# Flamingo block on one core: the split chain moves from VectorE to GpSimd, both norms' scales become one chain, and the second product's last tiles move one step on

## The reference, cut to what matters

```python
x = x + tanh(g_xattn) * xattn(layernorm(x), ctx, Wq, Wkv, Wout, bout)
x = x + tanh(g_ffn)   * ffn(layernorm(x), ln1_g, ln1_b, w1, b1, ln2_g, ln2_b, w2, b2)
# ffn: h = layernorm(x)*ln1_g + ln1_b ; h = bitlinear(h, w1, b1) ; h = gelu(h)
#      h = layernorm(h)*ln2_g + ln2_b ; h = bitlinear(h, w2, b2)
# bitlinear: the row is rounded to 8 bits with scale 127/max|row|,
#      w is rounded to -1, 0 or 1 with scale 1/mean|w|, then x @ w.T + b
```

## Time and profile before

| | |
|---|---|
| median of 3 executions | 404.12 us (401.83 to 404.73) |
| profiled execution | 403.77 us, span 401.9 us |
| VectorE, TensorE, ScalarE, GpSimd busy | 82%, 77%, 69%, 55% of the span |
| mean granted TensorE clock | 0.945 |

### The profile page before, as it was taken

The page is one execution under the profiler, slowest core; times in us unless marked ns, Lnnn a source line. Parts: engine busy times, 40 slices in busy tenths (PEclk is TensorE's granted clock), DMA queues, the critical chain, the costliest instruction groups (busy, mean ns, idle before and its releaser), DMA issues.

```text
span 401.9 us, 5821 instructions
## 1 busy us (share of the span) xinstructions
PE 309.3 (77%) x1690; PEld 189.8 (47%) x1690; DVE 328.1 (82%) x794; ACT 277.6 (69%) x446; POOL 220.9 (55%) x118
## 2 busy tenths in 40 slices
PE   2887586969797978888888888888879675848465
PEld 2675344435555555545454546464636342515143
DVE  0489237979999999999999999999999995968781
ACT  1214456869787878796969696969696967879340
POOL 4021163949292929393948484848484757565500
PEclk9999698969999999999999999999999996969688
DMA  7774413336282829191919282828170717252625
GB/s 226 231 238 172 131 52 81 104 58 133 74 208 76 214 66 223 55 229 59 229 60 213 76 195 95 182 106 174 62 155 31 140 44 114 72 111 73 157 55 155
DMA packets 97687, 51.56 MB, mean 128 GB/s; under 512 B 86536, under 2 KB 88769, under 8 KB 97655
## 3 DMA queue, kind: packets, MB, share of 16 engines
q1 hardware_dynamic: 96758, 51.14, 49.9%
q10 hardware_dynamic: 896, 0.04, 0.1%
HBM read 21.78 MB, written 8.41 MB: 75 GB/s over the span
## 4 chain that ended last, share of the span: by engine, by line
DVE 41%; PE 35%; issue 9%; POOL 7%; ACT 3%; DMA 3%; DVEq 0%; POOLq 0%; SPq 0%; ACTq 0%
DVE y L683 10%; PE bank_f L951 8%; POOL rstd L320 6%; PE slot_c L913 5%; DVE res L733 5%; DVE h L642 5%; DVE amax L650 5%; PE slot_a L939 4%; DVE amax L687 3%; PE bank_q L892 3%; PE slot_b L939 3%; DMA c_in<-in_ctx 3%; DVE x L599 3%; DVE parts L585 2%; PE slot_a L936 2%
## 5 line engine op out<-in xcount | busy, mean ns | idle before, releaser
L336 POOL TENSOR_TENSOR y<-u,g_bc 128x1024 f32<-128x1024 f32 x64 | 150.2, 2368 | 27.8 <-DVE parts L585 25.4
L320 POOL TENSOR_TENSOR rstd<-var,half_neg 128x8 f32<-128x8 f32 x18 | 29.5, 1641 | 99.1 <-DVE var L724 88.1
L683 DVE TENSOR_TENSOR y<-y,slot_c 128x1024 f32<-128x1024 f32 x64 | 77.6, 1212 | 5.3 <-PE slot_c L913 5.3
L687 DVE TENSOR_REDUCE amax<-y 128x1 f32<-128x1024 f32 x64 | 78.1, 1220 | 2.2
L427 ACT ACTIVATE q<-y,s 128x1024 f16<-128x1024 f32 x64 | 69.8, 1139 | 9.9 <-DVE s L714 9.8
L454 ACT ACTIVATE junk<-u,usum 128x1024 bf16<-128x1024 f32 x64 | 73.7, 1151 | 1.2
L951 PE MATMUL bank_f<-w2T,q2T 128*128 128x256 f16 x512 | 68.1, 281 | 2.0 <-DVE res L733 2.0
L892 PE MATMUL bank_q<-wvo,ctxT 128*128 128x256 f32 x240 | 64.6, 401 | 0.0
L951 PEld LDWEIGHTS bank_f<-w2T,q2T 128*128 128x128 f16 x512 | 51.4, 101 | 16.6 <-DVE res L733 2.9
L913 PE MATMUL slot_c<-ln_rows,rows 128*128 128x512 bf16 x128 | 41.5, 408 | 16.9 <-DVE y L683 8.4
L418 ACT ACTIVATE q<-h,s 128x256 f16<-128x256 f32 x64 | 27.3, 496 | 37.6 <-DVE s L674 37.5
(11 more groups left out here) (115 smaller groups left out, 407.9 us busy)
## 6 DMA issues: line engine op xcount, KB each, us to landing
c_in<-in_ctx SPq DMA_DIRECT2D x16, 512.0 KB, 3.3
x_in<-in_x SPq DMA_DIRECT2D x16, 512.0 KB, 4.2
out<-res SPq DMA_DIRECT2D x32, 256.0 KB, 2.6
y<-in_L_ffn_w SPq DMA_DIRECT2D x2, 1024.0 KB, 9.6
u<-in_L_xattn_Wkv SPq DMA_DIRECT2D x1, 1024.0 KB, 6.7
u<-in_L_xattn_Wout SPq DMA_DIRECT2D x1, 1024.0 KB, 10.4
q2T<-q SPq DMA_TRANSPOSE x64, 3.3
g_bc<-in_L_ffn_ln_g SPq DMA_DIRECT2D x1, 512.0 KB, 4.3
```

The source lines that it names most:

```text
L320: nc.gpsimd.tensor_tensor(rstd[:, :, :], var[:, :, :], half_neg[:, :, :], ALU.pow) \
L336: nc.gpsimd.tensor_tensor(y[:, k % 2, t, :], u[:, t, :], g2_bc[:, :], ALU.mult).then_inc(gain2_done, 1)
L683: nc.vector.tensor_tensor(line, line, slot_c[:, :], ALU.add).then_inc(y_done, 1)
L687: nc.vector.tensor_reduce(amax2[:, t:t + 1], y[:, k % 2, t, :], AX.X, ALU.max, apply_absolute_value=True).then_inc(amax2_done, 1)
```

## The change

- `variance`, `deviations` and `split` leave VectorE's program and stand in GpSimd's. GpSimd's body begins with `deviations` and the five steps of `split` and ends with `variance(i)` and `root(i + 1)`. `rstd` gets a second buffer. GpSimd's wait for the split steps ahead of its gains goes away with that, and only tile 3's `gain` stays one body later.
- `first` and `second` become one chain `scales` of six instructions over both norms (128x8 where it was 128x4), at the end of the body, with nothing between its dependent steps.
- `join` of set i+2 is cut into its four steps, which stand between `row` and `row_max` of tiles 0 and 1.
- `rows` is doubled. `take_rows` stands behind the first `quantise`.
- The second product's tiles 2 and 3 and their `final` run one body later; tiles 0 and 1 run behind `hidden(3)`.
- The second half of attention writes slot_b and is run at the end of the body before; TensorE turns the first half of the next context at the body's start.
- Body 0 has an order of its own, with `shift_first(1)` ahead of most of its products.

```diff
+                def variance(k):
+                    wait(pool, square_done, T * k + T)
+                    wait(pool, std_done, i + 2)
+                    wait(pool, split_steps, split_count(i))
+                    nc.gpsimd.tensor_scalar(stat[:, 2, :], usum[:, :], -1.0 / H, None, ALU.mult)
+                    nc.gpsimd.tensor_scalar(var[:, 1, :], usq[:, :], 1.0 / float(H) ** 3, LN_EPS,
+                                            ALU.mult, ALU.add).then_inc(var2_done, 1)
+                def split(n):
+                    if n == 0:
+                        wait(pool, std_done, min(i + 2, S + 2))
+                        wait(pool, join_steps, 3 * min(i + 2, S))
+                        wait(pool, scales_ready, scales_after(i - 1))
+                        wait(pool, rows_done, i + 1)
...
                 if -1 <= i <= S:
-                    root()
-                    wait(pool, split_steps, split_count(i))
+                    deviations()
+                if -1 <= i <= S + 1:
+                    for n in range(5):
+                        split(n)
...
                 if live(i - 1):
-                    gain(i - 1, 2)
                     gain(i - 1, 3)
                 if live(i + 1) and i > -1:
                     gain_first(i + 1)
                 if live(i):
                     gain(i, 0)
                     gain(i, 1)
+                    gain(i, 2)
+                    variance(i)
+                if -1 <= i + 1 <= S:
+                    root(i + 1)
```

VectorE, the join's new waits, the scale chain and the order of a steady body:

```diff
                     if n == 0:
-                        wait(dve, bn_done, 2 * k + 2)
-                        wait(dve, split_steps, split_count(k - 2))
+                        wait(dve, bn_done, k + 1)
+                        wait(dve, std_done, i + 2)
+                        wait(dve, split_steps, split_count(i))
...
+                def scales(kinds=slice(0, 2), those=slice(0, T)):
...
+                    nc.vector.tensor_tensor(amax_g[one], amax[one], power, ALU.mult) \
+                        .then_inc(scale_steps, 1)
...
+                    nc.vector.scalar_tensor_tensor(
+                        out=scale[one], in0=amax_inv[one], scalar=QMAX * TINY, in1=power,
+                        op0=ALU.mult, op1=ALU.mult).then_inc(scales_ready, 1)
...
                 if live(i - 1):
                     row(i - 1, 0)
+                    if live(i + 2):
+                        join(i + 2, 0)
                     row_max(i - 1, 0)
+                    if live(i - 3):
+                        final(i - 3, 2)
+                        final(i - 3, 3)
+                    if live(i + 2):
+                        join(i + 2, 1)
                     row(i - 1, 1)
+                    if live(i + 2):
+                        join(i + 2, 2)
                     row_max(i - 1, 1)
+                    if live(i + 2):
+                        join(i + 2, 3)
...
                     row(i - 1, 2)
                     row_max(i - 1, 2)
+                    row(i - 1, 3)
+                    row_max(i - 1, 3)
...
                 if live(i - 2):
                     final(i - 2, 0)
-                if live(i - 1):
-                    row(i - 1, 3)
-                    row_max(i - 1, 3)
+                    final(i - 2, 1)
                 if live(i + 1):
                     shift_first(i + 1)
...
+                if live(i + 1):
+                    first_max(i + 1)
+                    scales()
```

ScalarE and TensorE, a steady body:

```diff
                 if live(i - 2):
                     quantise(i - 2, 0)
...
+                if i > 0:
+                    take_rows()
+                if live(i - 2) and i <= S:
                     quantise(i - 2, 1)
...
-                if live(i + 2):
-                    attention(i + 2, 1)
...
+                if live(i + 3):
+                    turn_context(i + 3, 0)
+                if i <= S + 1:
                     turn_rows()
+                if live(i - 3):
+                    second_product(i - 3, 2)
                 if live(i - 1):
                     correction(i - 1, 0)
+                if live(i - 3):
+                    second_product(i - 3, 3)
                 if live(i):
                     hidden(0)
...
                 if live(i):
                     hidden(3)
+                if live(i - 2):
+                    second_product(i - 2, 0)
+                    second_product(i - 2, 1)
+                if i == S + 1:
+                    second_product(i - 2, 2)
+                    second_product(i - 2, 3)
                 if live(i + 1):
                     shift_first(i + 1)
-                if live(i - 2):
-                    second_product(i - 2, 1)
                 if live(i + 3):
                     attention(i + 3, 0)
+                    attention(i + 3, 1)
```

More of the change, by code:

```diff
@@ new lines, in final @@
+                def final(k, t):
+                    if t % 2 == 0:
+                        wait(dve, ffn_done, T * k + t + 2)
+                    if t == 0:
+                        wait(dve, stored[k % 2], 32 * (k // 2))
+                    nc.vector.scalar_tensor_tensor(
+                        out=res[:, k % 2, t, :], in0=bank_f[:, D * (t % 2):D * (t % 2 + 1)],
+                        scalar=d12[:, (k + 1) % 2, 1, t:t + 1], in1=x1[:, k % SETS, t, :], op0=ALU.mult,
+                        op1=ALU.add).then_inc(final_done, 1)
@@ L756, in body @@
                 if i == -1:
-                    deviations()
-                    for n in range(5):
-                        split(n)
                     residual(1, 0)
                     statistics(1, 0)
+                    statistics(1, 1)
                     round_weights(1, 1)
                     shift_first(0)
-                    for n in range(5):
-                        first(0, n)
+                    first_max(0)
+                    dve.wait_ge(wscaled, 2)
+                    scales()
                     residual(1, 1)
-                    statistics(1, 1)
+                    statistics(1, 2)
+                    statistics(1, 3)
                     for n in range(4):
@@ L770, in body @@
                     return
-                if live(i - 1):
-                    variance(i - 1)
+                if i == 0:
+                    shift_first(1)
+                    first_max(1)
+                    scales()
+                    residual(2, 0)
+                    statistics(2, 0)
+                    statistics(2, 1)
+                    residual(2, 1)
+                    statistics(2, 2)
+                    statistics(2, 3)
+                    for n in range(4):
+                        join(2, n)
+                    return
                 if live(i + 2):
@@ L775, in body @@
                     statistics(i + 2, 0)
-                if i <= S:
-                    deviations()
-                if i <= S + 1:
-                    for n in range(5):
-                        split(n)
-                if live(i - 3):
-                    final(i - 3, 1)
-                if live(i + 2):
-                    residual(i + 2, 1)
-                    statistics(i + 2, 1)
+                    statistics(i + 2, 1)
+                    residual(i + 2, 1)
+                    statistics(i + 2, 2)
@@ L796, in body @@
+                    row_max(i - 1, 3)
+                if i == S + 1:
+                    final(i - 3, 2)
+                    final(i - 3, 3)
                 if live(i - 2):
                     final(i - 2, 0)
-                if live(i - 1):
-                    row(i - 1, 3)
-                    row_max(i - 1, 3)
+                    final(i - 2, 1)
                 if live(i + 1):
                     shift_first(i + 1)
-                    first(i + 1, 0)
-                for n in range(4):
-                    if i == S:
-                        second(i - 1, n, slice(2, 4))
-                    elif live(i - 1):
-                        second(i - 1, n)
-                    if live(i + 1):
-                        first(i + 1, n + 1)
-                    if live(i + 2):
-                        join(i + 2, n)
+                if live(i + 1):
+                    first_max(i + 1)
+                    scales()
@@ L932, in hidden @@
                         wait(pe, rows_copied, i + 2)
+                    if t == 1 and i > 0:
+                        wait(pe, x1_done, 2 * min(i + 3, S))
                     wait(pe, gelu_done, T * i + t - 1)
```

330 lines of the change are left out of this document (150 added, 180 removed).

## The result

The changed kernel takes 462.54 us (458.92 to 464.70, four executions) against 404.36: a ratio of 1.146, 95% interval 1.142 to 1.151. The forecast was 449, with 425 to 470 around it. The profiled execution took 458.92 us with a span of 457.0, against 403.77 and 401.9 before: 55.1 us of span to be found.

The account below looks back on a forecast made before the run. VectorE was taken to bound the steady body, busy 19.30 of 20.55 us. Against 403.8: 13 bodies from 20.5 to 24.0 +45.5, start -3.4, bodies 14 and 15 -1.5, end +4.6 gives 449 us; range 425 to 470.

Parts of the forecast that it names:

- the case of three held joins: Steady body: three joins held by GpSimd's gains, body 24.0 us, time 449, own range 440 to 458; chance 0.62.
- the start: Up to set 0's first row: earlier splits and gelus put that row at 67.4 against 70.83, -3.4 us.
- bodies 14 and 15: Last two bodies: no join in them, so -1.5 us together.
- the end: From set 15's first row to the last finals: 26.7 us against 22.1, +4.6.
- three holds: Steady body: joins 0, 1 and 2 wait for GpSimd's products, 1.3, 1.6 and 1.4 us, together 4.3.
- the successor of L625: A sign in join 1: 1 us and more, ending with a GpSimd product, would show the prediction right.
- rival 2: Steady body: only some joins are held, join 1 slips ahead of gain 0, -1.5 us a body, 430; chance 0.12.
- VectorE's own work, 18.0: Steady body: VectorE's instructions without waits sum to 18.0 us, including 1.13 for the new scale chain.
- Five split steps: Start of GpSimd's body: the moved split takes 1.7 us, hidden, with 1.4 to 1.8 likely and 2.5 not excluded.
- Rival 3: GpSimd's small instructions are slow, 0.5 us each, rows 0.9 us a body late: 461, up to 470; chance 0.12.
- rival 1: Steady body: joins aren't held, body 19.7 to 19.9 us, time 395 to 397; chance 0.14.
- 18.0 + 0.9 + 0.8: Steady body without holds, 19.7 us: VectorE's work, 0.9 idle ahead of the first row, 0.8 ahead of the finals.

Follow-up runs that it names:

- probe_kinds: Kernel before, with one extra four-element VectorE instruction behind each of the first three `row_max` of bodies 2 to 13, six kinds by turns; 421.63 us, one execution.
- old_joins_in_rows: Kernel before, with only the joins moved into its rows, as they stand in the changed kernel; 489.15 us, ratio 1.212.
- joins_late: Changed kernel with the four join steps moved from the rows to behind `shift_first`; 412.02 us, ratio 1.023.
- start_and_end: Changed kernel with set 0's q1 transpose ahead of context 4's load on SyncE and the first correction ahead of both second products; 466.80 us, ratio 1.159.
- late_products_early: `joins_late` with the earlier q1 transpose and second products of tiles 2 and 3 at the end of their own body behind attention; 408.45 us, ratio 1.014.
- the last kernels: Late joins, early transpose, correction 1 ahead of `hidden(0)`: one with finals ahead of the first row (404.99 us), one with rows first and tile 3's product between corrections (403.47).

## Why the prediction was right, point by point

**The time.** 462.5 us is inside the stated range, 13 us above the 449 and above the 440 to 458 that the case of three held joins was given. The profiled execution's span grew by 55.1 us where the sum had 45.2: the start is 6.4 above its term, bodies 14 and 15 are 3.6, the 13 bodies 0.9, and the end is 1.0 below. The other 3.6 us are the median's distance from the profiled execution. The mechanism and the large term were right; two small terms were wrong in sign.

**The joins: right in cause and size.** The step said 1.3, 1.6 and 1.4 us for three holds, 4.3 a body; in the body shown they are 1.50, 1.60 and 1.58 beyond the 0.15 of a free instruction, 4.7; over the 13 bodies they add up to 60 us, 4.6 a body. Late joins give 50 us back, and the old kernel with the joins in its rows loses 86: that is shown from both sides. The choice hung on a single row, 0.55 us at 29.06 that ended with GpSimd's product. By the Trainium skill (SBUF — State Buffer, "Who interferes with whom") a VectorE instruction with two SBUF inputs is blocked by a GpSimd instruction that reads SBUF, if it comes later, and the trace agrees (1.65 us ending 0.02 us after the product).

**Details of it were wrong without cost.** The step had only instructions with two SBUF inputs held, and of join 1 that would be its second, L645. In fact L644 was held, a `tensor_scalar` with one input (1.75 us), and L645, the successor of L625 that the prediction named as a sign, then took 0.15; it is the same gain that holds, so the sum is the same. L654, which the step left free, was held for 1.79 in bodies in which it fell under gain 2 (176.65). The same section of the Trainium skill lists `tensor_scalar` and copies among the operations that can take both ports under conditions; `probe_kinds` shows them held at four elements, strided output included. The prediction also feared that a queued second gain could hold a join longer, and had none queued. A queued product doesn't keep a held instruction out, but three small instructions in a row need a gap (L620 of `old_joins_in_rows`, 2.33 us).

**Not every body has the same holds.** Join 1 slips in ahead of gain 0 in some bodies (172.17, 0.15), as rival 2 said. But what follows is then held longer, 2.16 and 1.79 us, so such a body is not 1.5 us shorter: 160.72 to 185.91 is the longer one of the two shown. Rival 2's price of -1.5 a body for one hold less was wrong.

**VectorE's own work, 18.0: 0.35 too much.** `joins_late` shows 17.65 busy, the wait ahead of the finals was 0.40, not 0.8, and the wait for the first row 0.84 against 0.9. These three are 0.8 us less than forecast and the holds 0.4 more, so the body shown is 23.7; the longer ones bring the mean to 24.1.

**GpSimd's small instructions: right.** Five split steps from 260.99 to 262.67 are 1.68 us (forecast 1.7, bounds 1.4 to 2.5). Rival 3 is out. That a root doesn't hold VectorE throughout, which the prediction took from one row, is seen many times: in `joins_late` the first instruction of the scale chain, with two SBUF inputs, started 14 times inside a root of 1.67 us, 0.2 to 1.3 us behind its start, and took 0.17 each time. Nothing waited for the root: it ends at 259.95, before the scale chain's end at 260.77.

**The start: wrong, 6.4 us.** The step had the gelus near 48 and the first row at 67.4. TensorE's timeline of the changed kernel, start and body 14:

```profile
50.35 0.58 PE L949 MATMUL slot_a<-b_rows,rows 128*128 128x512 bf16 x1 [3.96 <-DMA q1T<-q]
...
383.75 0.39 PE L913 MATMUL slot_c<-ident_b,parts 128*128 128x128 bf16 x2 [5.75 <-POOL parts L366]
383.93 1.92 PE L963 MATMUL bank_f<-w2T,q2T 128*128 128x256 f16 x8
...
385.85 1.06 PE L924 MATMUL slot_c<-ln_rows,rows 128*128 128x512 bf16 x2
```

The splits came at 45.99, as forecast (45.9), but `hidden(0)` waited 3.96 us for the transpose of q1, and the first gelu started at 53.10. The step had priced GpSimd and ScalarE and had left out SyncE's queue, where the transpose stands behind a load that waits for turned context. Putting the transpose first moved the row by 2.7 us (`start_and_end`). The rest, 3.7 us, came by attention. The step had set 3's attention end near 66 and the row 1.4 behind it; it ended at 72.2, and the row followed at 73.84 behind the residual and its statistics. That attention started at 66.44, behind ScalarE's copy of the context, and two of its four products ran at the lower clock, 1.74 and 1.92 us for 1.03. Two holds are seen as well, the scale chain's L698, 2.33 us at 56.81, and the join at 62.57, 1.67, but VectorE stood idle for 1.39 us ahead of that residual, so they may have cost nothing. How the 3.7 us divide is not shown.

**Bodies 14 and 15: wrong, 3.6 us.** They were taken for shorter since they have no join. They also have no attention and no residual, so VectorE and TensorE stand idle at their head until the splits come (5.75 us), then tile 2's second product runs ahead of the correction at the lower clock (1.92 us for 1.04), and the row waits. The lines show it for body 14, whose wait of 5.17 us lies just ahead of the cut and so in the 13 bodies; inside the stretch, the first rows of sets 14 and 15 wait 5.16 and 7.53 us, where before each waited 1.2 (for set 15 in the earlier trace rows). What the missing work saves is less than these waits: +2.1 us for the two bodies instead of -1.5. The step had counted VectorE's work and the loop over ScalarE, but not that with nothing else to do the whole path from the scale chain to the row is open. The end behind them was 3.6 instead of 4.6, by the forecast's mechanism: the last finals stand at 447.43, 450.54 and 453.65, each behind its own second product.

**What the change would be worth without the holds: rival 1 was too hopeful.** It said 395 to 397. `joins_late` is that kernel, and it takes 412. By the same cuts it has +1.8 at the start, -0.6 in 13 bodies where the rival had -9, and +7.2 from set 13's first row on. The 13 bodies get back 47 of the 60 us of holds; the rest went into the wait for the first row, about 2 us in most of them where it was 0.84. The rival had VectorE's 18.0 plus two waits of its own, and no loop over TensorE: at the start of a body TensorE is idle for 2.0 us (1.45 and 0.58), the granted clock then is 0.50 (from 212.9 to 216.3 us), and what is on the path now takes 1.8 times as long: the second product 1.88 for 1.04 and the correction 1.06 for 0.60, and in `late_products_early` the first hidden product 1.06 for 0.59. The windows of the last kernels give the price as a difference between bodies of one order: 19.7 us at 1.00, 20.8 to 21.3 at 0.92. That body of 19.7 is the prediction's "18.0 + 0.9 + 0.8" by other waits.

What stays open: why the clock falls in some bodies and not in others of the same order, and whether an order exists that keeps TensorE fed there.

## What to carry to other kernels

Before a small VectorE instruction is moved, look at what GpSimd runs at its new place: one of four elements can cost all that is left of a GpSimd product, the profile counts it as busy, and it ends with the product. If no gap is there for it, cut the GpSimd product in two: the overhead (0.13 us a product here) is less than what one hold shrinks by (1.65 to 0.71, 1.75 to 0.52). And when work leaves the bounding engine, price the path that becomes open beside it with TensorE at its lower clock, and every DMA queue on it too.

## What the runs showed of the hardware

- A four-element `tensor_scalar` or copy with a single SBUF input is held by a GpSimd product like one with two inputs: 2.34 and 2.36 us for 0.16, also with an output stride of two elements. `tensor_reduce` over 1024 elements (1.21 under gains) and instructions with an operand in PSUM (1.21 and 0.86) were not, nor was the reciprocal (0.17, six of six, two of them just behind a product's start).
- GpSimd's power on 128x8 (1.67 us) doesn't hold VectorE once it is under way: a 128x8 `tensor_tensor` with two SBUF inputs, started 0.2 to 1.3 us behind it, took 0.17, 14 times of 14 in `joins_late`.
- Of the held instruction and a GpSimd product already queued, the held one goes first, at the end of the running product, and the small one behind it got through too (0.15 us); the third was caught by the next product for its whole length (2.33).
- GpSimd's small instructions were cheaper than its 1.67 us power suggests: cast of 128x72 0.29 us, `tensor_tensor` of 128x24 0.25 to 0.27, `tensor_scalar` of 128x4 0.19 to 0.23. VectorE takes 0.20 to 0.22 for the first two.
- TensorE's granted clock was 1.00 in one body and 0.92 in the next with the same work and order, in kernels with idle times of 0.3 to 1.5 us at the body's head.
